# A signature, two attentions and two mixtures of experts in one kernel: the router of the last mixture in shorter steps, position queries placed by transfers, a running sum in two FP32R parts

## The reference, cut to what matters

```python
new.append(acc)                       # signature: levels summed over the steps
sigs = ...; return sigs @ W.T + b
...
attn1 = jnp.einsum('bhqd,bhkd->bhqk', rq, rk)
attn2 = jnp.einsum('bhqd,qkd->bhqk', rq, rk2)      # rk2 = rel_k[idx], clipped distance
attn = jax.nn.softmax((attn1 + attn2) * (1.0 / math.sqrt(c)), axis=-1)
...
scores = jax.nn.sigmoid(xf @ gate_w.T)
top_scores, top_idx = jax.lax.top_k(scores, K)
top_scores = top_scores / (top_scores.sum(-1, keepdims=True) + 1e-20) * ROUTE_SCALE
oh = jax.nn.one_hot(flat_e, E, dtype=jnp.int32)
pos = jnp.take_along_axis(jnp.cumsum(oh, axis=0), flat_e[:, None], axis=1)[:, 0] - 1
buf = jnp.zeros((E, CAP, d)).at[flat_e, pos].set(x_pairs, mode='drop')
```

## Time and profile before

| | |
|---|---|
| median of 3 runs | 2158.98 us (2153.92 to 2160.1) |
| profiled execution, its own time | 2159.81 us |
| its span | 2158.0 us, 59101 instructions |
| granted clock, mean | 0.913 |
| PE busy | 1747.0 us (81%), 21991 instructions |
| DVE | 1411.1 us (65%), 3365 |
| ACT | 926.8 us (43%), 2288 |
| POOL | 848.8 us (39%), 1748 |

### The profile page before, as it was taken

How to read it: one execution, slowest core, us unless ns; L and a number is a source line. 1 busy time by engine, 2 the same in 40 slices (tenths; PEclk the granted TensorE clock), 3 DMA queues, 4 the chain that set the end, 5 groups by cost and what they waited for, 6 DMA issues and landing times. The chain is left out here.

```text
span 2158.0 us, 59101 instructions
## 1 busy us (share of the span) xinstructions
PE 1747.0 (81%) x21991; PEld 1432.7 (66%) x21991; DVE 1411.1 (65%) x3365; ACT 926.8 (43%) x2288; POOL 848.8 (39%) x1748
## 2 busy tenths in 40 slices
PE   5999999999789739943999999999998996066660
PEld 4888888888577639942887777777777775033440
DVE  6777777777578746655677777777777775123334
ACT  2111111111376407732677666666666663022220
POOL 3333333333016556631012433434444445655551
PEclk9999999999899859975999999999999998588875
DMA  8900000000300012230233333333333332064427
GB/s 309 103 0 0 0 0 0 0 0 0 135 28 26 26 52 70 72 107 25 53 62 71 69 66 67 71 67 70 72 74 76 71 69 45 33 191 123 125 66 242
DMA packets 312522, 147.59 MB, mean 68 GB/s; under 512 B 205094, under 2 KB 291140, under 8 KB 311876
## 3 DMA queue, kind: packets, MB, share of 16 engines
q1 hardware_dynamic: 299732, 118.38, 23.8%
q0 software_dynamic: 12544, 25.91, 3.7%
HBM read 72.03 MB, written 73.37 MB: 67 GB/s over the span
## 5 line engine op out<-in xcount | busy, mean ns | idle before, releaser
L1808 ACT ACTIVATE rel_e<-rel_s_ps,rel_neg_max 128x255 f32<-128x255 f32 x512 | 199.9, 476 | 68.9 <-DVE rel_neg_max L2082 68.4
L495 PE MATMUL tok_main_ps<-tok_w_h,tok_feat_h 128*128 128x512 f32 x512 | 205.6, 402 | 0.9 <-DVE tok_feat_low L99 0.9
L495 PE MATMUL tok_main_ps<-tok_w_h,tok_feat_l 128*128 128x512 f32 x512 | 200.1, 391 | 0.0
L495 PE MATMUL tok_main_ps<-tok_w_l,tok_feat_h 128*128 128x512 f32 x512 | 199.7, 390 | 0.0
L2082 DVE TENSOR_REDUCE rel_neg_max<-rel_s_ps 128x4 f32<-128x1020 f32 x128 | 155.4, 1215 | 51.6 <-PE rel_s_ps L1597 50.0
L2053 DVE SCALAR_TENSOR_TENSOR rel_q_head_l<-rel_qT,all_k_mask,rel_q_head_h 32x256 fp32r<-32x256 f32 x256 | 112.3, 475 | 94.3 <-ACT rel_q_head_h L1799 92.0
L1616 PEld LDWEIGHTS rel_t_ps<-all_k_ident,rel_e 128*128 128x128 f32 x1024 | 110.6, 142 | 83.6 <-issue 80.0
L1616 PE MATMUL rel_t_ps<-all_k_ident,rel_e 128*128 128x128 f32 x1024 | 140.1, 280 | 29.4 <-DVE rel_work L2171 16.2
L84 POOL TENSOR_TENSOR tok_q_pre<-tok_v_q,tok_v 128x128 f32 (+1 forms) x32 | 39.2, 1225 | 312.3 <-DVE tok_q L269 298.0
L1583 PE MATMUL rel_s_ps<-rel_k_h,rel_q_head_h 128*128 128x256 f32 x512 | 155.9, 304 | 4.8 <-DVE rel_q_pos L2063 4.8
L296 DVE TENSOR_REDUCE tok_inc<-tok_prod 128x128 f32<-128x1024 f32 x64 | 128.8, 2012 | 34.9 <-PE tok_small_ps L511 33.8
(11 more groups left out here) (333 smaller groups left out, 4737.0 us busy)
## 6 DMA issues: line engine op xcount, KB each, us to landing
rel_q_rep<-q_rows SPq DMA_DIRECT2D x256, 64.0 KB
o_rows<-rel_rv SPq DMA_DIRECT2D x256, 64.0 KB
x_slots<-early_zeros SPq DMA_DIRECT2D x16, 520.0 KB, 6.5
exp_x<-x_slots SPq DMA_DIRECT2D x32, 260.0 KB, 2.9
y_rows<-early_zeros SPq DMA_DIRECT2D x16, 512.0 KB, 6.5
final_y<-y_rows SPq DMA_DIRECT2D x16, 512.0 KB, 10.1
exp_x<-x_slots SPq DMA_DIRECT2D x72, 65.0 KB, 1.8
rows_y<-y_rows SPq DMA_DIRECT2D x8, 512.0 KB, 6.5
```

The costliest lines, as they stand in the source:

```text
L495: nc.tensor.matmul(main_ps[s][:, cols], feat[fk][:, s, j, :], w_p[wk][:, j, cols], start=(j == 0 and (fk, wk) == (0, 0)), stop=False)
L1808: last = nc.scalar.activation(e[u % 2][:, n, 0:L], s_ps[u % 2][:, n, 0:L], ACT.Exp, bias=neg_max[u % 2][:, n:n + 1])
```

## The change

1. Signature: the increments are rounded on ACT (`increments`), DVE makes the remainder (`increment_remainder`), and the running sum is two FP32R products of 256 columns and two of 128 with an FP32R triangle. DVE's next reduction waits for that rounding instead of the sum.
2. Position queries: qT is stored as [128, place in the group of four, group]. SP writes it to DRAM with one transfer and eight transfers (pieces of 256 bytes) place it straight into `q_pos`, which POOL has zeroed once. `position_queries`, its mask and `q_rep` go. `position_scores` waits for the transfers, and the queries' readers read qT with every element 64 elements from the last.
3. Router: lags 2, 3, 4, 5 (rows, best two, choice, count and places). PE transposes rows at u3 and multiplies with the gate at u1, into places of the bank that DVE's `best` reads directly; ACT copies 256 columns at u3. The count goes from u3 to u1. At u1 PE waits for DVE's copy before count, logits and the projection of keys. ACT's `rows` go from the front of u0 to the end of u1. The sigmoid and its sum are all on DVE. POOL routes a chunk ahead of the factors of an even batch. The tail loops are two or three batches shorter.

```diff
-                        dve.wait_ge(h_ready, b)
+                        dve.wait_ge(inc_round, b)
...
+                def increment_remainder(b):
+                    dve.wait_ge(inc_round, b + 1)
+                    rest(nc.vector, inc_p[1][:], inc[:], inc_p[0][:]).then_inc(inc_rest, 1)
...
+                def increments(b):
+                    act.wait_ge(inc_ready, 2 * b + 2)
+                    if not isinstance(b, int) or b >= 1:
+                        act.wait_ge(h_ready, b)
+                    nc.scalar.activation(inc_p[0][:], inc[:], ACT.Copy).then_inc(inc_round, 1)
...
-                    nc.tensor.matmul(h_ps[:, 0, :], upto[:, 0:P], inc[:, 0, :], start=True, stop=True)
-                    nc.tensor.matmul(h_ps[:, 1, :], upto[:, P:T], inc[:, 0, :], start=True, stop=False)
-                    nc.tensor.matmul(h_ps[:, 1, :], upto[:, 0:P], inc[:, 1, :], start=False,
-                                     stop=True).then_inc(h_ready, 1)
+                    for k in range(2):
+                        nc.tensor.matmul(both, upto_r[:, 0:P], inc_p[k][:].rearrange("p s d -> p (s d)"), start=(k == 0),
+                                         stop=False)
+                    for k in range(2):
+                        last = nc.tensor.matmul(h_ps[:, 1, :], upto_r[:, P:T], inc_p[k][:, 0, :], start=False,
+                                                stop=(k == 1))
+                    last.then_inc(h_ready, 1)
...
-LAG_X, LAG_TOP, LAG_COUNT, LAG_PLACE = 3, 4, 6, 7
+LAG_X, LAG_TOP, LAG_CHOOSE, LAG_COUNT = 2, 3, 4, 5
...
         def of_pair(q, k):
-            return q[32 * k:32 * k + 32].rearrange("p (g i) -> p g i", i=QUAD)
+            return q[32 * k:32 * k + 32].rearrange("p i g -> p g i")
...
+                    sp.dma_start(q_rows[r], qT[:]).then_inc(q_out, 16)
+                    sp.wait_ge(q_out, 16 * b + 16)
...
-                            sp.dma_start(q_rep[at:at + HD],
-                                         q_rows[r][:, f].rearrange("(h d) u t -> d h (u t)", d=HD)).then_inc(q_in, 16)
+                            sp.dma_start(q_pos[r][at:at + HD, :, i], q_rows[r][:, i].rearrange("(h d) g -> d h g", d=HD))\
+                                .then_inc(pos_in[r], 16)
...
-                    if u == 2 and b >= LAG_X:
-                        pe.wait_ge(route_read, b - LAG_X + 1)
-                    if u == 0 and chunk_at(b - 1, LAG_COUNT) is not None:
-                        pe.wait_ge(work_ready, chunk_at(b - 1, LAG_COUNT) + 1)
+                    if u == 0 and b > LAG_X:
+                        pe.wait_ge(route_read, b - LAG_X)
+                    if u == 2 and b >= LAG_TOP:
+                        pe.wait_ge(top_ready, b - LAG_TOP + 1)
+                    if u == 2 and chunk_at(b, LAG_COUNT) is not None:
+                        pe.wait_ge(work_ready, chunk_at(b, LAG_COUNT) + 1)
...
-                    if u == 1 and have(b + 2):
-                        project_k(b + 2)
+                    if u == 1:
+                        pe.wait_ge(eT_v, NU * b + u + 1)
+                        route(b, u)
+                        if have(b + 2):
+                            project_k(b + 2)
...
-                    if u == 0 and LAG_X <= bb < B + LAG_X:
+                    if u == 1 and LAG_X <= bb < B + LAG_X:
                         rows(bb - LAG_X)
...
                 for b in range(B):
-                    q = chunk_at(b, LAG_COUNT - 1)
-                    if q is not None:
-                        add_one(q)
+                    if chunk_at(b, LAG_CHOOSE) is not None:
+                        route(chunk_at(b, LAG_CHOOSE))
                     factors(b)
-                    if q is not None:
-                        route(q)
...
-                        last = nc.vector.max(top[j][:, t0 + t], logits_of(b)[:, t])
+                        last = nc.vector.max(top[j][:, t0 + t], logit_ps[:, t])
...
-                    nc.vector.reciprocal(sig[:], one_more[:]).then_inc(sig_ready, 1)
+                    link(nc.vector.tensor_scalar(sig[:], odds[q % 2][:], 1.0, None, ALU.add))
+                    link(nc.vector.reciprocal(sig[:], sig[:]))
+                    link(nc.vector.tensor_tensor(sums[:], sig[:, 0], sig[:, 1], ALU.add))
+                    link(nc.vector.tensor_scalar(sums[:], sums[:], 1e-20, None, ALU.add))
                     nc.vector.reciprocal(over[:], sums[:]).then_inc(over_ready, 1)
...
                 def route(bb, u):
-                    if u == 2:
+                    if u == 1:
                         if LAG_TOP <= bb < B + LAG_TOP:
                             best(bb - LAG_TOP)
                         if chunk_at(bb, LAG_COUNT) is not None:
-                            choose_second(chunk_at(bb, LAG_COUNT))
-                        if chunk_at(bb, LAG_PLACE) is not None:
-                            places(chunk_at(bb, LAG_PLACE))
-                            over_sums(chunk_at(bb, LAG_PLACE))
+                            weigh(chunk_at(bb, LAG_COUNT))
+                    if u == 2:
+                        if chunk_at(bb, LAG_CHOOSE) is not None:
+                            choose_first(chunk_at(bb, LAG_CHOOSE))
+                        if chunk_at(bb, LAG_COUNT) is not None:
+                            places(chunk_at(bb, LAG_COUNT))
+                            scores(chunk_at(bb, LAG_COUNT))
                     if u == 3:
-                        if chunk_at(bb, LAG_PLACE) is not None:
-                            accumulate(chunk_at(bb, LAG_PLACE))
-                        if chunk_at(bb, LAG_COUNT - 1) is not None:
-                            choose_first(chunk_at(bb, LAG_COUNT - 1))
+                        if chunk_at(bb, LAG_CHOOSE) is not None:
+                            choose_second(chunk_at(bb, LAG_CHOOSE))
                         if chunk_at(bb, LAG_COUNT) is not None:
-                            scores(chunk_at(bb, LAG_COUNT))
-                            weigh(chunk_at(bb, LAG_COUNT))
+                            accumulate(chunk_at(bb, LAG_COUNT))
```

206 lines of the change are left out of this document (100 added, 106 removed).

## The result

| | before | changed |
|---|---|---|
| median | 2159.54 us (4 runs) | 2223.45 us (4 runs) |
| ratio, 95% interval | | 1.0302 (1.0282 to 1.0321) |
| span of the profiled execution | 2158.0 us | 2221.9 us |

The account below looks back on a forecast made before the run. PE was taken to bound the signature and lead the attention, sharing its path with other engines. Attention +60, tail -22, head -6 and signature -7 gave +25 us on 2159.81: 2185, range 2112 to 2212.

Parts of the forecast that it names:

- Signature, head, tail: Running sum, -7 us; start of attention without L2063, -6; router's last chunks, two routes left, -22.
- The attention: Rounds of two batches: four steps sum to 4.4 us more a round, over 13.5 rounds +60 us.
- The price of the strided reads: Head queries reading qT strided: .18 to .20 us an operation on DVE, half of 0 to .2 on ACT.
- (2): Slots u1: PE waits for DVE's copy first, cover lost, query operations longer: +1.3 us each, +2.6 a round.
- (4): Even batch's slot u3: rows, stride and ACT's wait for POOL, less relieved DVE and PE cover: +.9 us a round.
- (1): Slots u0: the stall on L2171 goes, copies come later: -.5 us each, -1.0 a round.
- (3): Odd batch's slot u3: ACT's rows, DVE's score operations, stride and later k_h, less PE's cover: +1.9 us a round.
- Rival A: Head queries' stride is free: attention +22 us, total -13, 2147 us; chance .17.
- Rival B: DVE's relief in the attention wins, slack absorbs stride and rows: 2089 us, or 2125 if losses cancel gains; chance .24.
- Rival C: ACT pays the stride in full, PE's weight loads too: about +46 us in all, 2206; chance .13.
- Rival D: The change's DMA transfers of position queries are late; said to change nothing, small chance counted within Rival C.
- The sign of being wrong: Attention round under 52.6 us, or head queries at .48 us, would show the forecast wrong.

Follow-up runs that it names:

- e1: Changed kernel with head queries reading qT in the order in which it lies, without the stride: 2162.66 us, ratio 1.0011.
- e2: Kernel before with only the head queries' reads of qT made strided: 2240.88 us, ratio 1.0384.
- E0: Not a run: slot u0 of a round's even batch (E even, O odd, digit the slot); 6.41 us before, 6.34 in the changed kernel.
- e4: Changed router and running sum with the position queries of the kernel before (natural qT): 2168.98 us, ratio 1.0044.
- e17: e4's kernel with ACT's router rows moved to the end of u2, behind the query rounding: 2118.46 us, ratio 0.9803.
- e14: e4's kernel with DVE's scores moved to the end of the odd u1: 2174.06 us, ratio 1.0066.

## Why the prediction was right and wrong

**Signature, head, tail: right.** -8.6, -3.9 and -22.0 for -7, -6 and -22. The -7 is nearer than it looks, since the sum itself gives 6.7. The .67 us that I took for the old sum are too much, as the first L495 starts .58 us behind it (at 309.43); the 7.4 us for short products paced by their loads are 6.9 by their own numbers. At the head the gain of -7.4 is there in e1, and the strided reads, which I had left out there, take 3.5 us of it back. The tail is two routes, as in the earlier trace rows for three:

```profile
1915.40 0.24 POOL L2010 TENSOR_SCALAR rel_valid<-rel_place 128x8 f32<-128x8 f32 x1 [0.37 <-DVE rel_place L2192]
1930.39 0.27 POOL L2010 TENSOR_SCALAR rel_valid<-rel_place 128x8 f32<-128x8 f32 x1
1943.29 0.96 POOL L2035 DMA_INDIRECT x_slots<-rel_x,rel_at  x1 [0.30 <-issue]
```

**The attention: the step that failed.** The sum had 4.4 us a round over 13.5 rounds, +60 us. It measured +96.0: 5.9 us a round, and 21.4 in the first three rounds. e1 parts it. The strided head queries, which had 2.8 us a round, 38 in all, take 56 (893.9 less e1's 837.5 us). The rest, which had 1.6 a round, 22 in all, takes 40 (e1's 837.5 less 797.9). So half of the error is the stride's and half the moved work's. The direction and most of the mechanisms were right; the terms were mis-sized, as follows.

**The price of the strided reads.** I put DVE at .18 to .20 us an operation (measured .185) and ACT at half of 0 to .2 (measured .255, above my bound). An upper bound taken from DVE was used for ACT, for which no row existed. On the path I let 2.8 us a round of both count, in the steps (2) to (4); e1 against the changed kernel shows 3.6, e2 against before 5.5. The Trainium skill ("Advanced Engine Details and Errata", section "SBUF Cachelines") states the penalty, without an engine or a price; the traces agree, with .185 us an operation on DVE and .255 on ACT, and the loads of `q_pos` on PE went from 106 to 194 ns. Those loads I put at nothing, up to .36 us a batch. They lengthen the position scores: 143.3 us before, 157.3 in the changed kernel, .44 a batch. Whether that was on the path of the changed kernel no run shows.

**The number of rounds.** I left out 2.5 rounds because the first batches route no chunk. But the head queries of every batch are strided, and the shorter lags bring the router's work into earlier rounds: in e1, without the stride, the first three rounds grow by .1, 4.1 and 4.7 us.

**(1) The slots u0: wrong.** I had -.5 each and no stride there. The stall on L2171, which stands at the end of E3, did go, and E3 is 1.41 us shorter; but O0 is 1.32 longer and E0 unchanged (-.07). ACT's six pieces in u3 take 4.34 us and stand ahead of the copy and the exponentials of u0. Against the run e1 the stride costs .82 in E0 and .80 in O0, 1.6 us a round that my sum had at nothing.

**(2) The slots u1: nearly right**, +1.43 and +1.77 for +1.3 each.

**(3) The odd u3: right**, O2 and O3 together +1.94 for +1.9.

**(4) The even u3: a right mechanism at the wrong time.** Since the stall lies in E3 too, (1) and (4) are read together: E0, E2, E3 and O0 sum to +.82 us where I had -.1. The wait for POOL, which I put at 1.5 us, isn't there in the changed kernel between 1200 and 1700 us: the rows start 21.0 to 21.6 us behind the place, and POOL is through in 20.3 to 20.5. In e4 and e1, without the stride, it is there and sets the round. That my two slots of rows at 1.0 and 1.5 of POOL are 3.5 a round and e17 takes away 3.6 is in part luck: 2.8 of it is the even u2 alone, and the odd u2 and u3 give .6. And I counted the wait as a stall in one slot beside others; it is a loop, so what is gained elsewhere is given back there (e14).

**Rival A** (stride free) had 1.6 a round over before and 2147 us; e1, the kernel without the stride, has 2.3 and 2162.66. So even that case was 16 us too low. **Rival B** (DVE's relief wins) is out: DVE's copy is waited for more, not less, in the changed kernel and, without the stride, in e1. **Rival C** (ACT pays in full, and PE's loads) was the nearest: 2206 of 2223 (2210 by its own terms), with a chance of .13 that was too small. Its half on ACT is what the runs show; its half on PE is open, as said above. **Rival D** is out: PE shows no wait for the placed queries. The sign of being wrong should have read 53.3 us a round and not 52.6, since 50.7 and 2.6 are 53.3.

## What to carry to other kernels

A layout that saves a transfer or a product is paid at every reader: count the readers and every batch in which they read, price each engine's read apart, and where no row shows an engine's price, take the dear case to be as likely as the cheap one. When a step that is moved closer to its use runs through a slow engine and comes back, add up the whole way round: if that is as long as a round of the loop, it isn't a stall in a slot but the bound, and other gains go into it. A step with slack of its own belongs behind the work that others wait for; here two lines, with the order of two operations on ACT and one on PE, turned 2168 us into 2105.
